# Reordering the seam between the gate projection and the state rows of a Mamba-2 mixer

## The reference

```
x = x + 0.5 * ffn(layernorm(x))      # 8 routed experts, top 2, and a shared one
x = x + mixer(layernorm(x))
x = x + 0.5 * ffn(layernorm(x))
```

```
z, xBC, dt = split(u @ W_in.T)                  # 1024, 1280 and 16 columns
xBC = silu(causal_conv4(xBC) + conv_b)          # depthwise, 4 taps
x, B, C = split(xBC);  dt = softplus(dt + dt_bias)
state_t = exp(-dt*A) * state_{t-1} + dt * x_t B_t^T        # from a state of zeros
y_t = C_t state_t + D * x_t
y = y * silu(z);  y = y * rsqrt(mean(y*y) + eps) * norm_w
out = y @ W_out.T
```

## Time and profile before

| | |
|---|---|
| median of 3 runs | 1554.17 us (1553.82 to 1558.59) |
| the profiled execution | 1555.85 us |
| its span | 1553.9 us |
| mean granted clock of TensorE | 0.982 |
| PE, PEld, DVE, ACT, POOL busy | 96%, 82%, 66%, 50%, 52% of the span |
| the mixer | 513 to 1046 us of the span |

### The profile page before, as it was taken

How to read it: one execution, slowest core, us unless ns; L and a number is a source line. 1 busy time by engine, 2 the same in 40 slices (tenths; PEclk the granted TensorE clock), 3 DMA queues, 4 the chain that set the end, 5 groups by cost and what they waited for, 6 DMA issues and landing times. The chain is left out here.

```text
span 1553.9 us, 22772 instructions
## 1 busy us (share of the span) xinstructions
PE 1492.2 (96%) x8450; PEld 1275.8 (82%) x8450; DVE 1033.3 (66%) x1762; ACT 772.4 (50%) x1335; POOL 808.1 (52%) x490
## 2 busy tenths in 40 slices
PE   6999999999999999999998999999999999999999
PEld 6878999999877787777777878778778999999877
DVE  7573656666466888687777867767754656666465
ACT  3313666666512556555565555643215666666311
POOL 2102777776454437535644743662015777776442
PEclk9999999999999999999999999999999999999999
DMA  7032778867453120021011011005034778876253
GB/s 303 28 119 82 264 253 276 274 241 267 170 173 107 50 84 4 14 70 40 1 56 67 1 39 44 17 22 183 28 112 155 270 250 283 282 266 236 73 174 124
DMA packets 70717, 213.78 MB, mean 138 GB/s; under 512 B 8080, under 2 KB 8080, under 8 KB 69712
## 3 DMA queue, kind: packets, MB, share of 16 engines
q1 hardware_dynamic: 48528, 154.66, 28.4%
q0 software_dynamic: 11360, 37.23, 8.0%
q10 hardware_dynamic: 10720, 20.45, 3.7%
HBM read 179.28 MB, written 33.03 MB: 137 GB/s over the span
## 5 line engine op out<-in xcount | busy, mean ns | idle before, releaser
L609 POOL TENSOR_TENSOR g_lo<-g_raw,g_hi 128x1408 fp32r<-128x1408 f32 x54 | 179.0, 3316 | 122.8 <-ACT g_hi L766 120.5
L609 POOL TENSOR_TENSOR u_lo<-u_raw,u_hi 128x1408 fp32r<-128x1408 f32 x54 | 174.2, 3226 | 61.7 <-ACT u_hi L766 61.7
L1739 PE MATMUL bank<-u_hi,xgT 128*128 128x352 f32 x624 | 168.5, 333 | 0.0
L1739 PE MATMUL bank<-g_hi,xgT 128*128 128x352 f32 x624 | 163.5, 324 | 0.0
L1762 PE MATMUL bank<-d_hi,hT 128*128 128x512 f32 (+1 forms) x468 | 159.5, 395 | 3.6 <-DVE hT L1087 3.6
L639 POOL DMA_INDIRECT xg<-token_x,row_of x78 | 86.8, 1112 | 138.3 <-DVE row_of L1232 121.7
L698 POOL TENSOR_TENSOR w_hl<-w_raw,w_hl 128x1024 fp32r<-128x1024 f32 x35 | 85.8, 2451 | 120.8 <-ACT w_hl L766 120.8
L815 ACT ACTIVATE gate<-bank 128x512 f32<-128x512 f32 (+1 forms) x48 | 28.6, 596 | 219.7 <-PE bank L1692 219.7
L1707 PE MATMUL bank<-d_hi,hT 128*128 128x512 f32 (+1 forms) x384 | 127.3, 405 | 3.6 <-DVE hT L1087 3.0
L1437 DVE SCALAR_TENSOR_TENSOR acc<-pre,cw,acc 128x512 f32<-128x512 f32 x120 | 125.2, 1043 | 4.3
L1692 PE MATMUL bank<-xs,g_hi 128*128 128x512 f32 (+1 forms) x384 | 122.5, 403 | 3.2 <-issue 1.5
(11 more groups left out here) (260 smaller groups left out, 3693.0 us busy)
## 6 DMA issues: line engine op xcount, KB each, us to landing
g_raw<-in_w_gate SPq DMA_DIRECT2D x54, 704.0 KB, 5.9
u_raw<-in_w_up SPq DMA_DIRECT2D x54, 704.0 KB, 6.7
d_raw<-in_w_down SPq DMA_DIRECT2D x54, 512.0 KB, 5.0
w_raw<-in_w_in SPq DMA_DIRECT2D x36, 512.0 KB, 3.5
routed_y<-ys ACTq DMA_DIRECT2D x32, 512.0 KB, 4.5
d_raw<-in_w_down SPq DMA_DIRECT2D x54, 192.0 KB, 5.5
token_x<-xn SPq DMA_DIRECT2D x8, 1024.0 KB, 5.6
X<-in_x SPq DMA_DIRECT2D x4, 1024.0 KB, 9.7
```

What stands on the lines that cost most here:

```text
L609: pool.tensor_tensor(half_of(piece, 1, s), raw_at[piece][s % RING][:], half_of(piece, 0, s).bitcast(F), ALU.subtract)\
L1739: ins = pe.matmul(dst[:, 0:FE], xgT[:, n % 2, hx, kc], half_of(piece, hw, NS + j)[:, kc], start=(m == 0), stop=(m == 3 * KD - 1))
```

## The change

- **Order of the units.** `ORDER = (0, 1, 2, 3, 5, 4, 6, 7, 8)`: z's first unit is the fifth of a block, between the convolution's channels 7 and 8. ACT's silu of channels 8 and 9 now stands in z's third unit.
- **DVE in the unit stage.** Softplus follows channel 5 (before: 7), `log1p` channel 7 (9), and `sums_by_row` with the copies of the sums channel 8 (9). The sums are copied in one piece (`sums`), `d_p` is taken from the copy, `ncs` is gone. `decay_sums` stands between the halves of unit 6.
- **Seam inside z's last unit.** PE issues the first row's `decays` of groups 0 and 1 ahead of unit 8's first half and its `products` (B by C and the transposes of x) ahead of the second half, which is written to bank 2. ACT clamps groups 0 and 1 in unit 7, ahead of unit 8's `unit_hi`, and takes the silu of the last half at the end of the first row. Row 0's exps come behind the copy of `GB`; its copy of the transposed next rows (`rows_hi`) stands ahead of groups 2 and 3.
- **Statistics.** The layer norm's statistics and roots of rows 0 and 1 are made together before the first row, not one per row. In row 0 of a block DVE scales the next row behind `xdt`, and makes the state's part of y between groups 1 and 2 of the products; POOL makes `xw` first and the old state second.
- **No empty state.** The zeroing is gone. Row n = 0 has no product with the state, writes `xD` straight to `y` and copies the new state from PSUM. Row n = 7 makes no new state; half of the projection of row 6 stands ahead of its product with the state, half behind it, and DVE makes the state's part of y behind the fourth product.

The core of the diff:

```diff
-CS_UNIT = 8
+ORDER = (0, 1, 2, 3, 5, 4, 6, 7, 8)
+CS_UNIT = (6, 1)
@@ POOL
-                            if u == 1 and j == 0:
-                                zero_state()
                         next_rows(0)
+                        next_rows(1)
                         for q in range(TB):
+                            def old_state():
+                                if 0 < n < TPB - 1:
+                                    after(m_C, n - 1, TPB - 1)
+                                    after(m_S, n, TPB - 1)
+                                    pool.tensor_tensor(S[:, (n + 1) % 2]..., S[:, n % 2]..., each(dec[:, hq], HD), ALU.mult).then_inc(m_Sd, 1)
+                            if q:
+                                old_state()
+                            if n < TPB - 1:
+                                (xw = xdt * wd)
+                            if not q:
+                                old_state()
                             if q >= 1:
                                 rms(n - 1)
-                            if q + 1 < TB:
+                            if 1 <= q < TB - 1:
                                 next_rows(q + 1)
+                            if n:
+                                (y = y + xD)
-                            after(m_z, 8 * (j + 1), 8 * BPB)
+                            after(m_z, 8 * (j + 1) - (q < 2), 8 * BPB)
@@ ACT
+                                for half in range(2 if u < NWU - 1 else 1):
+                                    z_out(j, u, half)
+                                    if u == 7:
+                                        conv_out(j * NCH + NCH - 2 + half, NCH - 2 + half)
+                                    if (u, half) == (7, 1):
+                                        clamp(j * TB, 0)
+                                        clamp(j * TB, 1)
@@ ACT, rows
+                            if q == 0:
+                                act.activation(wd[:], d_p[:], ACT.Exp)
+                                act.activation(dec[:], tot, ACT.Exp)
+                                act.activation(ecs[:], pcs, ACT.Exp).then_inc(m_dec, 1)
                             decay(n, 0)
                             decay(n, 1)
+                            if q == 0:
+                                rows_hi()
+                            else:
                                 squares(n - 1)
+                            for g in range(2, HG):
+                                clamp(n, g)
+                                decay(n, g)
+                            if q == 0:
+                                z_out(j, NWU - 1, 1)
+                            else:
+                                rows_hi()
@@ DVE
+                            if c == NCH - 5:
+                                softplus()
                             if c == NCH - 3:
-                                softplus()
-                        log1p()
-                        sums_by_row()
+                                log1p()
+                            if c == NCH - 2:
+                                sums_by_row()
+                                after(m_cs, j + 1, BPB)
+                                own.step(dve.tensor_copy(sums[:], bank[2][:, NQ:3 * NQ]))
+                                dve.tensor_tensor(d_p[:], tot, pcs, ALU.subtract).then_inc(m_sums, 1)
                         next_stats(0)
+                        next_stats(1)
@@ DVE, rows
+                            decayed(0)
+                            decayed(1)
+                            if q == 0:
+                                from_state()
+                            elif q + 1 < TB:
+                                next_stats(q + 1)
+                            decayed(2)
+                            decayed(3)
+                            if n == TPB - 1:
+                                from_state()
+                            if q:
                                 residual(n - 1)
+                            if q and n < TPB - 1:
+                                from_state()
@@ PE
+                        for p, u in enumerate(ORDER):
...
+                                    if (u, half) == CS_UNIT:
+                                        decay_sums()
+                                    if (u, half) == (NWU - 1, 0):
+                                        decays(j * TB, 0, 0)
+                                        decays(j * TB, 0, 1)
+                                    if (u, half) == (NWU - 1, 1):
+                                        products(j * TB)
+                                        after(m_sums, j + 1, BPB)
+                                    place = 2 if (u, half) == (NWU - 1, 1) else 6 + half
@@ PE, rows
+                                project(n - 1, range(2) if n < TPB - 1 else (0,))
+                            if n:
+                                (C by the state, m_C)
+                            if n == TPB - 1:
+                                project(n - 1, (1,))
+                            if n < TPB - 1:
+                                (Bt by xw, m_D)
```

More of the change, by code:

```diff
@@ L998, in turn @@
                                     after(m_yg, 2 * j * TB, 2 * TPB)
-                                for half in range(2):
-                                    n = j * 8 + (u - 5) * 2 + half
-                                    after(m_zp, n + 1, 8 * BPB)
-                                    act.activation(zs[:, 2 * half:2 * half + 2, (u - 5) * WU:(u - 4) * WU],
-                                                   bank[6 + half][:].rearrange("p (q n) -> p q n", q=2),
-                                                   ACT.Silu).then_inc(m_z, 1)
@@ L1566, in turn, with from_state @@
-                            ins.then_inc(m_yc, 1)
+                            def from_state():
+                                if n:
+                                    after(m_C, n, TPB - 1)
+                                    after(m_dec, j + 1, BPB)
+                                    after(m_F, 2 * (n - 1), 2 * TPB)
+                                    after(m_sq, n - 1, TPB)
+                                    for half in range(2):
+                                        hs = slice(half * DI // 2, (half + 1) * DI // 2)
+                                        ins = dve.tensor_tensor(heads_of(y[:, n % 2, hs]), heads_of(bank[6 + half][:]),
+                                                                each(ecs[:, q * HEADS + half * HB:q * HEADS + (half + 1) * HB],
+                                                                     HD), ALU.mult)
+                                        if half == 0:
+                                            own.mark(ins)
+                                    ins.then_inc(m_yc, 1)
@@ L1887, in y_features, with project @@
                             ins.then_inc(m_F, 1)
-                    def project(n):
+                    def project(n, halves=range(2)):
                         if n % TB == 0:
@@ L1893, in project @@
                             pe.wait_ge(m_wo_lo1, 2)
-                            after(m_dec, n // TB + 1, BPB)
+                            after(m_z, 8 * (n // TB + 1), 8 * BPB)
                         after(m_res, n, TPB)
-                        m = 0
-                        for half in range(2):
+                        for half in halves:
                             after(m_ylo, 2 * n + half + 1, 2 * TPB)
+                            m = half * 3 * KI // 2
                             for c in range(4 * half, 4 * half + 4):
```

279 lines of the change are left out of this document (138 added, 141 removed).

## The result

| | before | after |
|---|---|---|
| median | 1555.10 us (4 runs, 1553.82 to 1558.59) | 1542.48 us (4 runs, 1539.76 to 1546.79) |
| ratio | | 0.9913, 95% interval 0.9887 to 0.9939 |
| profiled execution, its span | 1555.85, 1553.9 | 1540.35, 1538.6 |

By the ratio the change is worth 13.5 us, with 9.5 to 17.6 as its ends; 15.2 were forecast.

A forecast was written before the change was run, and what follows sets the result against it. PE, busy 96% of the span, bounds the kernel. First blocks 2 x 5.2, second blocks 2 x 0.3, row 7 3.2, less 0.6 for table loads, plus 1.6 of clock: 15.2 us, so 1539; range 1520 to 1549.

The forecast's parts named there:

- the clock: PE's slow stretches behind stalls: up to 1.7 us per seam, 2.5 in the fourth block, of which 1.6 counted as won.
- Unit order: z's first unit fifth: its 2.79 us silu wait goes; new waits of 0.7, and 2.3 (or 0.1) at the sums.
- Seam: From channel 9's end, silu, clamps and the next block's unit_hi and unit_lo run beside PE's own work until 712.1.
- T: End of POOL's low half for the next block's first unit, at the seam; forecast 712.1 in the earlier trace's times.
- Behind T: POOL's next_rows and xw follow, delaying the first row; second blocks' y matmuls start at T + 8.0, netting 0.3 us won.
- both collisions: Second blocks' first row: POOL's old_state holds back two products of L with GB, its y + xD the fourth.
- First blocks: Row 0 of each batch's first block, without state work: gain 5.6 us, taken as 5.2 after 0.4 lost next row.
- Row 7: Last row of a batch makes no new state: 1.6 of 1.72 us won, twice, 3.2 in all.
- Table switches: ACT's two extra 1.28 us loads per block cost 0.6 us in all; rival, held twice as long: 1545, chance 0.06.
- PE bound: Rival: collisions fall elsewhere and PE is never held before the third z unit's end; 1526 to 1527, chance 0.24.
- The ports take it all: Rival: second blocks lose 2 us each, first win 2 less, clock drops remain or double; 1551, no change, chance 0.12.
- The three things: PE's mixer waits per block: z's first silu 2.8 us, first-row clamps 2.4, y times the state 0.8.

The follow-up runs named there:

- e2: The change with the decay sums' matmuls half a z unit later, ahead of unit 7's first half; 1540.63 us, ratio 0.9888 to the kernel before.
- e1: The kernel before with the empty-state part alone, its unit order, seam and statistics kept; 1546.85 us, ratio 0.9946 to the kernel before.
- e7: The change with z's last half unit copied without silu, so two table loads per block go; 1542.52 us, ratio 0.9919 to the kernel before.
- e9: The change with decay sums half a unit later, POOL's next-block low half in the third row, ACT's high half ending the first; 1526.71 us, ratio 0.9805.
- e8: The change with POOL's low halves cut to an eighth of their columns, except the first two units; 1522.31 us, ratio 0.9779 to the kernel before.
- e10: The change with the first row's products issued behind z's last half unit; 1548.56 us, ratio 0.9941 to the kernel before.

## Why the prediction was right, and where its working was not

Right in sign, in size (1539 for 1542.5, well inside the range) and in the main in mechanism, with one term mis-sized, the clock. With the shift of 6.41, step by step in the second block:

- **Unit order.** The wait for z's silu is gone, and 0.7 was forecast for the low half: 0.67 (3.9 over four blocks, up to 1.7). `log1p` was to be blocked at the third instruction from its end; it was the last but one, to the same effect: end forecast at 689.8, seen at 689.75, PE's wait 2.3 forecast, 2.24 seen, 8.7 in four. Channel 9 forecast at 699.6, seen at 699.50.
- **Seam.** T was forecast at 705.7 and came at 707.28. The term that failed is the clock: the working ran PE at full rate behind the new stall, except for 0.9 us that it left in the fourth block. After the 2.24 us PE ran at 0.66, the 72 z matmuls took 9.84 us for 3 x 3.03, the sums' matmuls 0.5 more than in e2, and z's third unit ended at 700.65 instead of 699.1. ACT takes that unit's silu before channel 9's, so the 1.5 us went straight into T. The third block shows what the clock alone did, for there it held behind the same stall: the 72 matmuls took 8.87, and T (836.25, the end of a subtraction of 2.40 us) came 65.90 us after the block's start, 1.3 sooner than the second block's 67.18 and 0.3 from the forecast of 65.6. e2 takes the stall away; there the low half ends at 704.95, 2.3 earlier than in the change.

```profile
820.20 0.54 PE L1970 MATMUL bank<-tri_b,aparts 128*96 128x128 bf16 x6 [2.24 <-DVE aparts L1494]
...
820.75 8.87 PE L2076 MATMUL bank<-w_hl,xs 128*128 128x256 f32 x72
```

- **Behind T the waits held.** y matmuls at T + 8.0: 715.28 forecast, 715.29 seen, with both collisions (the pair 2.88 for 1.29, the second 3.43), and the next row's end 1.9 late. But the y matmuls took 5.46 us up to the next row's first matmul (720.75) for the 4.6 of the working (T + 8.0 to T + 12.6), and for 4.30 in e2, where the clock held: the clock again, 1.2 us.
- **First blocks.** Forecast 5.2 each, seen 3.5 and 4.2. PE waited for `xw` before D by 1.66 and 1.82, as forecast (some 1.5), and the next row lost 0.5 and 0.9 for the 0.4 taken.
- **Row 7.** 1.6 forecast, 1.55 seen, twice. **Empty state as a whole:** e1's 8.4 us, so most of the gain; the forecast did not price this part by itself.
- **Table switches.** e7: no more than the measurement can tell, so the 0.6 stays unproven. The Trainium skill (ScalarE: Activation LUTs, What ACT_TABLE_LOAD costs) counts a drain of 1.38 us with each load; the trace again leaves no room for one on either side (ACT, second block of the change: the activation ends at 713.43, the load begins at 713.45 and ends at 714.73, and the silu begins at 714.74):

```profile
712.80 0.63 ACT L984 ACTIVATE L<-L 128x512 f32<-128x512 f32 x1
713.45 1.28 ACT L991 ACT_TABLE_LOAD   x1
714.74 0.60 ACT L991 ACTIVATE zs<-bank 128x512 f32<-128x512 f32 x1
```

- **Rivals.** *PE bound* (1526 to 1527) did not happen, and its price was not tested by itself. e9 and e8 reached 1526.7 and 1522.3, but by other edits; e2, which takes away the same stall, brought 3.9 us for the 12.5 that this rival put on it, as part of it came back as other waits. *The ports take it all* happened in the second block alone, a loss of 2.4 us against 2 forecast, by the clock rather than by one more collision.

- **Reading of the waits.** The three things called almost all that PE waits for are 24.2 of the 33.6 us in that view. Its third line, which the earlier trace rows doesn't show, is the wait for y before its transposes; the change left it at 5.3, and no term of the sum rested on it.

```profile
PE bank L1885 <- POOL y L746: 4.2, 14, 0.8
```

**The size of the clock term.** By the traces' record of the granted clock PE was at the 1.2 GHz level for 23.9 us of the mixer before and for 20.5 after, so the change won some 1.7 us by it. The working let the old seam's stretch go in each block (1.7 each) and won 1.6 more in the fourth, some 8.4 in all. The 6.7 between the two are more than the 3.9 that is missing in the mixer.

Open: why the clock fell behind some of these stalls and not behind others. It fell behind three of the change's four waits for the sums (1.98 to 2.24 us), and behind none of the four in e10, which are as long. e9 wins 7 us by moving 1.05 us of ACT's work in each of four blocks, up to half of it by the clock; no run here sets the clock by itself. Nor does a run undo the statistics or VectorE's new places alone.

## What to carry to other kernels

A stall of two us that the working has found may cost more than its length, by the clock: here 1.4 us more in the z stage of the second block and 1.2 in its y matmuls, and nothing behind the same stall for the sums in the third block or in e10. So give it a range, from nothing to the cost of such a stretch in the trace, and not the one or the other. When a helper engine's big element-wise operation blocks the vector engine, ask of each instance which due time it has: the one ahead of the seam was due a whole stage later, and moving it, its producer and the sums took the gain from 13.5 us to 30. Look for the slot in the blocked engine's timeline and not in the helper's, for in the wrong row the same move lost 6 us.

## What the runs showed of the hardware

VectorE stood still for POOL's `tensor_tensor` in operations with a single SBUF input too, not only in those with two, and for the whole of it: in e2 the cast of `aparts` began at 687.21 beside a subtraction of 687.06 to 689.46.

```profile
687.21 2.37 DVE L1494 CAST aparts<-d_a 128x192 bf16<-128x192 f32 x1
...
692.84 1.85 DVE L1505 CAST cs_rows<-xD 32x256 bf16<-32x256 f32 x1
```

The same casts take 0.26 and 0.28 us in the trace of the change. The working had left casts out. The Trainium skill (GPSIMD Engine Reference, 1. Specifications) has them in: by it the two engines contend where VectorE has two SBUF inputs or runs in a mode that uses both ports for one. These rows agree if the casts run in such a mode, which no run here shows. ScalarE hardly felt POOL, by one pair of rows: the silu of a half unit took 0.66 beside the subtraction at 704.89 and 0.60 without one.
